# First expert's down tiles of the first batch: four in a row, or two and two with an up unit between

## What is computed

```python
x = x + attention(folded_condition(x))                     # block 1
x = x + routed_ffn(expert_of_condition(x))                 # block 2

def expert_of_condition(x):                                # one expert of 8 per batch
    expert = argmax(cond_8, axis=-1)
    up, gate = x @ W_up[expert].T + b_up, x @ W_gate[expert].T + b_gate    # 256 -> 512
    return (silu(up) * gate) @ W_down[expert].T + b_down                  # 512 -> 256

def routed_ffn(h):                                         # per token: 2 experts of 8
    logits = h @ Wg.T
    top_v, top_i = top_k(logits, 2)
    pos = cumsum(onehot(top_i)) - 1       # place in the expert's list; 640 places each
    ...                                   # gather rows by list, expert MLP, weigh, add back
```

## Time and profile before

| | |
|---|---|
| median of the timed runs | 930.89 us |
| the profiled execution | 926.78 us, its span 925.5 us |
| TensorE (PE) busy | 911.2 us, 98% of the span |
| VectorE (DVE) busy | 528.7 us, 57% |
| ScalarE (ACT) busy | 444.4 us, 48% |
| GpSimd (POOL) busy | 269.8 us, 29% |
| chain that ended last | PE 89%, DVE 4%, issue 2%, DMA 2%, ACT 2%, POOL 1% |
| granted TensorE clock | 9 (90% or more) in each of 40 slices, mean 1.000 |

### The profile page before, as it was taken

The page is one execution under the profiler, slowest core; times in us unless marked ns, Lnnn a source line. Parts: engine busy times, 40 slices in busy tenths (PEclk is TensorE's granted clock), DMA queues, the critical chain, the costliest instruction groups (busy, mean ns, idle before and its releaser), DMA issues.

```text
span 925.5 us, 13114 instructions
## 1 busy us (share of the span) xinstructions
PE 911.2 (98%) x4859; PEld 767.9 (83%) x4859; DVE 528.7 (57%) x975; ACT 444.4 (48%) x827; POOL 269.8 (29%) x242
## 2 busy tenths in 40 slices
PE   8999999999999999999999999999999999999998
PEld 4768868887799999998888888888888888888886
DVE  6754454578757766785665564333333335688544
ACT  3665566434355455572343343343343442345775
POOL 1533321310475765653400152041140230010000
PEclk9999999999999999999999999999999999999999
DMA  8030001220445343432503013003003011000011
GB/s 301 30 114 23 24 1 69 104 81 28 121 129 157 125 126 126 126 125 77 180 18 148 12 24 137 0 1 137 1 8 129 1 55 83 1 0 1 1 46 46
DMA packets 22192, 67.47 MB, mean 73 GB/s; under 512 B 4514, under 2 KB 11954, under 8 KB 19314
## 3 DMA queue, kind: packets, MB, share of 16 engines
q1 hardware_dynamic: 16546, 40.15, 11.9%
q0 software_dynamic: 5440, 26.50, 9.9%
q10 hardware_dynamic: 144, 0.00, 0.0%
HBM read 55.09 MB, written 9.45 MB: 70 GB/s over the span
## 4 chain that ended last, share of the span: by engine, by line
PE 89%; DVE 4%; issue 2%; DMA 2%; ACT 2%; POOL 1%; SPq 0%; ACTq 0%; DVEq 0%; POOLq 0%
PE banks L1112 18%; PE banks L1114 18%; PE banks L1113 18%; PE banks L1365 5%; PE banks L1367 5%; PE banks L1366 5%; PE banks L1206 3%; PE banks L1190 3%; PE banks L1404 2%; PE banks L1403 2%; PE banks L1197 2%; PE banks L1417 1%; PE banks L1416 1%; PE banks L1160 1%; DMA weight_stage<-in_cond_w 1%
## 5 line engine op out<-in xcount | busy, mean ns | idle before, releaser
L1112 PE MATMUL banks<-input_hi,mlp_hi 128*128 128x512 f32 x376 | 147.6, 392 | 0.0
L1114 PE MATMUL banks<-input_hi,mlp_lo 128*128 128x512 f32 x376 | 146.4, 389 | 0.0
L1113 PE MATMUL banks<-input_lo,mlp_hi 128*128 128x512 f32 x376 | 146.4, 389 | 0.0
L1631 ACT CAST hidden_hi<-hidden 128x512 fp32r<-128x512 f32 x96 | 59.6, 621 | 158.6 <-DVE hidden L2048 107.5
L2237 POOL TENSOR_TENSOR mlp_lo<-weight_stage,mlp_hi 128x768 fp32r<-128x768 f32 x32 | 59.1, 1846 | 172.4 <-ACT mlp_hi L1609 172.4
L2054 DVE TENSOR_TENSOR hidden_lo<-hidden,hidden_hi 128x512 fp32r<-128x512 f32 x96 | 66.4, 692 | 61.7 <-ACT hidden_hi L1631 61.4
L2048 DVE SCALAR_TENSOR_TENSOR hidden<-banks,L_expert_weight,gelu 128x512 f32<-128x512 f32 x64 | 48.0, 750 | 83.6 <-PE banks L1114 80.5
L1625 ACT ACTIVATE gelu<-banks 128x512 f32<-128x512 f32 x96 | 57.4, 598 | 71.2 <-PE banks L1114 63.5
L1114 PEld LDWEIGHTS banks<-input_hi,mlp_lo 128*128 128x128 f32 x376 | 70.6, 188 | 14.8
L1113 PEld LDWEIGHTS banks<-input_lo,mlp_hi 128*128 128x128 f32 x376 | 70.6, 188 | 14.4
L1112 PEld LDWEIGHTS banks<-input_hi,mlp_hi 128*128 128x128 f32 x376 | 70.6, 188 | 14.2
(11 more groups left out here) (350 smaller groups left out, 2148.8 us busy)
## 6 DMA issues: line engine op xcount, KB each, us to landing
weight_stage<-in_packF SPq DMA_DIRECT2D x8, 1536.0 KB, 7.0
weight_stage<-in_shared SPq DMA_DIRECT2D x2, 3072.0 KB, 11.2
expert_output<-y_rows SPq DMA_DIRECT2D x40, 128.0 KB, 1.8
weight_stage<-in_cond_w SPq DMA_DIRECT2D x4, 512.0 KB, 5.3
residual<-in_xT SPq DMA_DIRECT2D x4, 512.0 KB, 10.7
first_half_swapped<-first_half SPq DMA_DIRECT2D x16, 128.0 KB, 2.0
routed_input<-x_rows SPq DMA_DIRECT2D x16, 128.0 KB, 1.7
weight_stage<-in_ffn_w SPq DMA_DIRECT2D x2, 1024.0 KB, 7.1
```

The costliest lines, as they stand in the source:

```text
L1112: pe.matmul(o, wh, dh, start=(i == 0), stop=False)
L1113: pe.matmul(o, wh, dl, start=False, stop=False)
L1114: last = pe.matmul(o, wl, dh, start=False, stop=(i == len(terms) - 1))
L1631: act.copy(hiD[n % 4][:, :], prod_t[n % 2][:, :]).then_inc(done)
```

## The change

In the loop of `all_chunks`, up unit 2 of chunk c is laid behind the second down tile, and the up units behind the down tiles begin at 3:

```diff
                 down(c - 1, t)
                 rows_of(c - 1, t)
                 yield
+                if t == 1:
+                    yield from up_units(c, 2, 3)
             if c == 2:
                 inverse(0)
             dve.append(("first", c - 1))
             between = routed_behind_first(c - 1)
-            yield from up_units(c, 2, HT, between)
+            yield from up_units(c, 3, HT, between)
             yield from between
```

## The result

The changed kernel took 936.22 us, the median of 6 executions (933.74 to 938.73), beside 931.16 us for the kernel before (930.61 to 931.75, 6 executions): ratio 1.0055, 95% interval [1.0043, 1.0067]. It is slower by 5.1 us. The forecast was 935.0 us, with a range of 933.2 to 936.8. Its spread, 5.0 us, is over four times that of before, 1.1 us. Three of its executions had a mean granted TensorE clock of 1.000 (933.74, 935.44 and 935.70 us), the other three 0.998 or 0.996 (936.73 to 938.73 us).

What follows compares the result with a forecast made beforehand. TensorE, busy 911.2 of 925.5 us, was taken as the bound. Two count waits, +5.28 us, less the bank waits, 1.16, gave +4.12 us; 930.89 + 4.1 = 935.0 us, range 933.2 to 936.8.

Steps and rivals of the forecast that it cites:

- The added wait: At the counts of chunks 0 and 1, TensorE waits behind unit 3 for the marks: 2.64 us each, 5.28 us.
- The bank waits: Down tile 3 of chunks 0 and 1 no longer waits for its bank: 0.68 and 0.48 us, minus 1.16 us.
- What moved: Casts, subtractions, `wg`, `first`, stores, weight fetch and `split_expert(0)` land elsewhere in the routed stretch, each at cost 0.
- `first` was in time: On VectorE, `first` of chunk 0 ends about 189.3 us, before `prod0` is due at 189.45: cost 0, at most 1.2 us.
- `split_expert(0)` ahead of unit 3 in chunk 3: Starting two yields earlier, it puts two casts ahead of `silu` of chunk 3's unit 3: cost 0, at most 0.3 us.
- The give-back: Rival: the wait for the last token list, 1.51 us, absorbs part of the delay, giving 933.5 us; chance 7%.
- The clock: Rival: TensorE's clock falls in the two new pauses, costing 5.2 us in all, giving 940.2 us; chance 4%.
- a granted clock of 1.00: Sign for the profile after: TensorE's granted clock stays at 1.00, the level of 2.4 GHz.
- the expert phase begins about 4 us later: Sign for the profile after: the expert phase's first spins, at 239.65 us before, begin about 4 us later.

Runs made afterwards that it cites:

- the count covered: Changed kernel with the count and its places moved into up unit 0 of the next chunk: 927.13 us beside 926.45 for before, ratio 1.0006.
- spins: Changed kernel with 10 spin matmuls ahead of the counts of chunks 0 and 1: ratio 1.0055 against before, and again 1.0046.
- marks late: Kernel before, four down tiles in a row, only the marks moved from up unit 2 into unit 3: 933.45 us beside 926.45, ratio 1.0071.
- each half: Change made in one turn of the loop alone, other turn as before: 932.81 us (first) and 934.20 us (second) beside 930.93, ratios 1.0019 and 1.0034.

## Why the prediction was right

- **The added wait, 2.64 us twice.** 2.64 measured in the profile after, from terms that hold one by one: 0.52 us from the last matmul to `prod0` for 0.53, 2.01 from `prod0` to the marks for 2.00, and 0.34 from there to the count for 0.34. The reason is shown by two runs: with the marks in unit 3 and the tiles untouched the waits are there, with `prod0` behind the marks most of them is gone; and with the count covered they are gone whole.
- **The bank waits, minus 1.16 us.** Both are gone from the profile after. With the clock kept up by spins the sum is 4.0 to 4.1 us for the 4.12 predicted.
- **What moved.** `wg` stands between two down tiles and takes 1.85 us as before. The casts and GpSimd's subtractions come as a 2 and a 4:

```profile
180.35 1.14 ACT L1530 CAST expert_hi<-weight_stage 128x512 fp32r<-128x512 f32 x2 [1.71 <-DMA weight_stage<-in_pack,rows_of_L_cond]
...
184.04 2.18 ACT L1530 CAST expert_hi<-weight_stage 128x512 fp32r<-128x512 f32 x4
...
181.06 2.55 POOL L2194 TENSOR_TENSOR expert_lo<-weight_stage,expert_hi 128x512 fp32r<-128x512 f32 x2 [3.25 <-ACT expert_hi L1530]
184.74 5.02 POOL L2194 TENSOR_TENSOR expert_lo<-weight_stage,expert_hi 128x512 fp32r<-128x512 f32 x4 [1.13 <-ACT expert_hi L1530]
```

One instruction of `first` was held, for 1.21 us, ending at 189.80 where the last subtraction ends at 189.76; by the rule of the Trainium skill, SBUF — State Buffer, "Who interferes with whom", the trace agrees, as the instruction has two SBUF inputs. `prod0` still waited 0.24 us for TensorE, so `first` was in time, where the forecast had 0.15 us to spare. `split_expert(0)` ahead of unit 3 in chunk 3 cost nothing: the change of time is the same at the counts of chunks 1, 2 and 3 in the profile after (6.69, 6.67, 6.67 us).
- **The give-back** at the last token list (a rival, 7%) didn't come: the wait is 1.5 us before and after.
- **The clock** is the step that failed. The forecast had it at 1.00 throughout and gave its fall 4%, as a case of all or nothing worth 5.2 us. It was neither. The mean clock was under 1.000 in 3 of 6 executions of the result and in 8 of 11 later ones, and in the three profiles of the changed kernel the 0.50 stands at one pause or both, at 1.5 to 1.7 us for 3.4 us at 0.50. The reason given against it (the pauses are shorter than the one at the start, with dense matmuls on both sides) was no evidence: the only pause in the trace of before that said anything was one of 1.5 us. TensorE: Matmul & The Clock Gate, of the Trainium skill, describes in "HAM oscillation — how this bites in real kernels" a clock that falls again at each wait between bursts of matmuls. The traces agree in part: 0.50 at four of the six pauses of 2.5 us in these three profiles. The waits of the page's kernel are longer, about 3 to 5 us, so only the measurement could say that 2.5 us are enough.
- **Luck.** That the median lay in the range owes something to chance. It depends on how many of the executions have a fall, half of them here: the three without lie at a median of 935.44 us. In the two later sets the changed kernel was 6.3 and 5.7 us over before; put on 930.89 us that is 937.2 and 936.6, the first of them outside the range. One of the signs named ahead, a granted clock of 1.00, was wrong. Another, that the expert phase begins about 4 us later, was not met either, at 6.67 us; by the stretch with spins its mechanism holds.

## What to carry to other kernels

When a generator is advanced once per unit of a loop, taking a unit out of the loop moves every step behind it: write out each engine's order around the change and look for an in-order engine that now reaches a wait while the chain it waits for stands behind its own last product. The price is then the whole chain. Two ways out were measured here: to lay the waiting step one unit later, behind other work, or to put the chain ahead of the unit's own last product on its engine. Count a pause of TensorE of the size seen here, 2.5 us, as the pause plus a good chance of the lower clock (at 7 of 10 such pauses here, some 1.6 us for each 3.4 us at 0.50), and compare kernels by the stretch between two events as well as by the median, as other parts of an execution differ by more than such a change: here the experts' phase by 3 to 5 us.

## What the runs showed of the hardware

- Of ten pauses of 2.5 us between dense matmuls in the profiles (six in the changed kernel, two with the marks late, one in each half) seven had a granted clock of 0.50 at them: for 3.4 us six times and 6.8 us once. It fell between 0.4 us ahead of the pause's end (second profile of the changed kernel) and 1.7 us behind it (marks late). With 10 spins that left 0.2 us of idle time the mean clock was 1.000 in all 10 executions. At the 1.5 us pause ahead of the last `inv` none of the 14 profiles shows a fall. Behind the wait for gelu, 1.8 us, one of four does.
- What a fall costs: 3.4 us at 0.50 made the stretch 1.5 and 1.7 us longer than with spins, 10.2 us at 0.50 made it 4.7 us longer.
- A 128x32 instruction of VectorE with two SBUF inputs, 0.19 us by itself, took 0.73 to 1.22 us beside GpSimd's 128x512 subtractions.
- In three of the sets the kernel before took 926.5 to 927.0 us, in the others about 931, and the variants moved with it. It isn't the chip: one chip gave 930.93 and later 927.00. In the profiles 3 to 5 us of difference lie in the experts' phase, 155.0 to 155.3 us against 158.3 to 160.3, of which the wait for gelu is at most 1.8; what causes it is open.
